# Selective-scan kernel: which engine weights each state, in a plan per scan order, and how y is laid out for two of them

## The reference, cut to what matters

```python
xs = jnp.stack([x_hw, x_wh, x_hw[..., ::-1], x_wh[..., ::-1]], axis=1)
delta = jax.nn.softplus(dts + dt_b[None, :, :, None])
def step(h, xs_t):
    d_t, u_t, B_t, C_t = xs_t
    dA = jnp.exp(d_t[..., None] * A)
    h = h * dA + (d_t * u_t)[..., None] * B_t[:, :, None, :]
    y = jnp.einsum('bkdn,bkn->bkd', h, C_t)
    return (h, y)
ys = ys[:, 0:2] + ys[:, 2:4, :, ::-1]
y = ys[:, 0] + ys[:, 1].reshape(Bb, Dd, Ww, Hh).transpose(0, 1, 3, 2).reshape(Bb, Dd, L)
```

## Time and profile before

| | us |
|---|---|
| median of 3 runs | 14696.03 |
| lowest and highest run | 14689.11, 14702.75 |
| the profiled execution | 14691.09 |
| its span | 14689.3 |
| PE, DVE, ACT, POOL busy in it | 13181.2, 12970.4, 11123.1, 10326.6 |

### The profile page before, as it was taken

The page is one execution under the profiler, slowest core; times in us unless marked ns, Lnnn a source line. Parts: engine busy times, 40 slices in busy tenths (PEclk is TensorE's granted clock), DMA queues, the critical chain, the costliest instruction groups (busy, mean ns, idle before and its releaser), DMA issues.

```text
span 14689.3 us, 247142 instructions
## 1 busy us (share of the span) xinstructions
PE 13181.2 (90%) x65256; PEld 8153.8 (56%) x65256; DVE 12970.4 (88%) x13833; ACT 11123.1 (76%) x22914; POOL 10326.6 (70%) x4126
## 2 busy tenths in 40 slices
PE   6888988889888998889988899888998889988899
PEld 4566455664556645566455664556645566455654
DVE  8999689996899978999689996899969999599995
ACT  5888578885788857887578876788767887678875
POOL 6999069980699807998079970899708996099960
PEclk9999999999999999999999999999999999999999
DMA  3443023430343303443033430344303442043420
GB/s 114 129 131 124 25 93 128 130 124 21 97 130 129 119 21 102 130 141 103 21 111 128 140 96 21 116 130 138 91 21 123 131 138 83 21 131 128 138 78 26
DMA packets 907982, 1468.60 MB, mean 100 GB/s; under 512 B 38912, under 2 KB 891904, under 8 KB 893664
## 3 DMA queue, kind: packets, MB, share of 16 engines
q1 hardware_dynamic: 906560, 1452.37, 31.2%
HBM read 1350.07 MB, written 102.17 MB: 99 GB/s over the span
## 4 chain that ended last, share of the span: by engine, by line
PE 33%; issue 24%; POOL 16%; DVE 15%; ACT 7%; DMA 2%; DVEq 1%; ACTq 1%; POOLq 0%; SPq 0%
POOL area L1794 12%; DVE area L1229 9%; PE ps L756 7%; PE ps L1030 5%; PE ps L1042 5%; DVE area L1257 4%; PE ps L743 3%; POOL area L1804 3%; PE ps L734 3%; ACT ps L1554 3%; DMA area<-bc_rows 2%; PE ps L892 2%; ACT area L1523 2%; PE ps L724 2%; PE ps L856 1%
## 5 line engine op out<-in xcount | busy, mean ns | idle before, releaser
L1229 DVE TENSOR_TENSOR_SCAN area<-ps,hst,area 128x384 f32<-128x384 f32 x9216 | 8581.8, 994 | 150.5 <-ACT ps L1554 69.6
L1794 POOL TENSOR_TENSOR area<-area 128x1152 f32<-128x1152 f32 x3072 | 7998.3, 2638 | 62.6 <-POOL area L1779 29.4
L1554 ACT ACTIVATE ps<-area,a_neg 128x384 f32<-128x384 f32 x9216 | 5259.7, 580 | 984.8 <-DVE area L1229 959.2
L756 PE MATMUL ps<-area,ident 128*128 128x384 f32 x11472 | 4127.3, 494 | 441.5 <-POOL area L1804 408.2
L756 PEld LDWEIGHTS ps<-area,ident 128*128 128x128 f32 x11472 | 2050.0, 191 | 1918.6 <-POOL area L1804 449.4
L743 PE MATMUL ps<-ident,area 128*128 128x128 f32 x20736 | 2882.2, 275 | 0.0
L743 PEld LDWEIGHTS ps<-ident,area 128*128 128x128 f32 x20736 | 2604.0, 192 | 50.3 <-ACT area L1523 1.5
L1523 ACT ACTIVATE area<-ps,area 128x384 f32<-128x384 f32 x3456 | 1972.6, 571 | 560.2 <-PE ps L734 559.4
L1714 ACT ACTIVATE area<-ps,t_neg,area 128x768 f32<-128x768 f32 x1728 | 1617.8, 986 | 1001.1 <-PE ps L1030 1001.1
L1774 POOL TENSOR_TENSOR area<-area,ones 128x2304 f32<-128x2304 f32 x16 | 85.2, 5352 | 3103.5 <-ACT area L1483 2980.9
L734 PE MATMUL ps<-ident,area 128*128 128x128 f32 x10368 | 1765.2, 279 | 326.4 <-ACT area L1523 314.0
(11 more groups left out here) (163 smaller groups left out, 9539.6 us busy)
## 6 DMA issues: line engine op xcount, KB each, us to landing
area<-bc_rows SPq DMA_DIRECT2D x1536, 768.0 KB, 6.7
xz<-x_normed SPq DMA_DIRECT2D x144, 288.0 KB, 6.3
area<-in_x SPq DMA_DIRECT2D x18, 1728.0 KB, 10.1
area<-x_padded SPq DMA_DIRECT2D x24, 1250.0 KB, 12.1
z_raw<-z_st SPq DMA_DIRECT2D x144, 192.0 KB, 6.2
area<-z_raw SPq DMA_DIRECT2D x8, 3456.0 KB, 14.9
x_padded<-x_st SPq DMA_DIRECT2D x120, 200.0 KB, 7.8
x_normed<-area SPq DMA_DIRECT2D x9, 1728.0 KB, 8.1
```

What stands on the lines that cost most here:

```text
L756: m = e.matmul(ps[:, 5 + j, 0:CH], ident[:], hb[:, i % NH, j], start=i == 0, stop=i == N - 1)
L1229: e.tensor_tensor_scan(rev(hb[:, i % NH, j], k), rev(ps[:, 2 + j, 0:CH], k), rev(dbu[:, i % NH, j], k), hst[:, i, j:j + 1], ALU.mult, ALU. ...
L1554: e.activation(ps[:, 2 + j, 0:CH], dlt[:, par, j], ACT.Exp, scale=a_neg[:, j, k, i:i + 1]).then_inc(da, 1)
L1794: e.tensor_tensor(dbu[:, i % NH], du[:, par], row_b[:, q % 2, i % ROWS:i % ROWS + 1].broadcast_to([128, J, CH]), ALU.mult).then_inc(dbus, 1)
```

## The change

The plans are new. `FIVE` (GpSimd 0, 3, 6, 9; turned 1, 4, 7, 10, 13) served orders 0 and 1; now order 1 has `SIX`, in which state 3 is turned and GpSimd has 0, 6, 9. Orders 0 and 2 have `LATE`: GpSimd 0, 6, 11; turned 1, 3, 4, 7, 10, 12, 13; so VectorE has 2, 5, 8, 9, 14, 15, and the units stand at 12 and 13 in place of 10 and 14, or 10 and 13. Order 3 keeps `SEVEN`, with GpSimd 0, 6, 9, the same turned states and VectorE 2, 5, 8, 11, 14, 15. In a late plan the x unit waits until the third delta tile has left bank 1 (dp_v), and the z unit waits for the x unit's copy-out (unit_ev).

In a slot with two tiles, the sums of GpSimd states now follow the first tile in place of leading. What was last in a slot, the add of y, and a unit that stands at 13, are done ahead of the second tile (`between`). Waits that named states 5, 8 and 11 or 8 follow the plan (`after_ln`, `ln_free`). The column orders' `y_chunk` and `y_psum` give (row, column) in place of (column, row): the SBUF side has runs of eight elements, and the PSUM side steps by 48.

```diff
@@ -72,12 +72,16 @@
         self.sum_at = {n: n + 3 for n in pool} | {n: n + 2 for n in self.dve}
         self.order = tuple(sorted(self.sum_at, key=self.sum_at.get))
         self.unit_after = tuple(max(n for n in self.dve if n < m - 1) for m in units)
+        self.late = units[0] > 11
+        self.ln_free = max(n for n in self.dve if n < 10)
+        self.after_ln = {5: 1, 8: 2, min(n for n in self.dve if n > 10): 3}
         self.np, self.nd, self.nt, self.ns = len(pool), len(self.dve), len(self.tiles), len(self.order)
 
 
-FIVE = Plan((0, 3, 6, 9), (1, 4, 7, 10, 13), (10, 14))
+SIX = Plan((0, 6, 9), (1, 3, 4, 7, 10, 13), (10, 14))
 SEVEN = Plan((0, 6, 9), (1, 3, 4, 7, 10, 12, 13), (10, 13))
-PLANS = (FIVE, FIVE, SEVEN, SEVEN)
+LATE = Plan((0, 6, 11), (1, 3, 4, 7, 10, 12, 13), (12, 13))
+PLANS = (LATE, SIX, LATE, SEVEN)
 assert 0 in PLANS[0].pool and all(p.order[0] == 0 and p.dve[:3] == (2, 5, 8) for p in PLANS)
 
 
...
@@ -483,12 +488,12 @@
 
             if k % 2 == 0:
                 return y_v[:, :, ds(pos(k, c), CH)]
-            return y_v.rearrange("p j (h w) -> p j w h", h=H)[:, :, ds(c * 8 if k < 2 else (NC - 1) * 8 - c * 8, 8), :]
+            return y_v.rearrange("p j (h w) -> p j h w", h=H)[:, :, :, ds(c * 8 if k < 2 else (NC - 1) * 8 - c * 8, 8)]
 
         def y_psum(k):
 
             p = ps[:, 5:8, 0:CH]
-            return p if k % 2 == 0 else p.rearrange("p j (w h) -> p j w h", w=8)
+            return p if k % 2 == 0 else p.rearrange("p j (w h) -> p j h w", w=8)
 
 
         @block.sync
@@ -762,33 +767,54 @@
                     if at:
                         turned_sum(q, at - 1)
 
-                def slot(q, m):
+                def slot(q, m, between=None):
 
                     p = plan(q)
-                    for i in p.order:
-                        if p.sum_at[i] == m and i in p.pool:
-                            state_sum(q, i)
+                    sums = [i for i in p.order if p.sum_at[i] == m]
+                    if len(p.slots[m]) < 2:
+                        for i in sums:
+                            if i in p.pool:
+                                state_sum(q, i)
                     for at in p.slots[m][:1]:
                         tile(q, at)
                     if m == N + 1:
                         turned_sum(q, p.nt - 1)
-                    for i in p.order:
-                        if p.sum_at[i] == m and i in p.dve:
+                    for i in sums:
+                        if i in p.dve or len(p.slots[m]) == 2:
                             state_sum(q, i)
+                    if between:
+                        between()
                     for at in p.slots[m][1:]:
                         tile(q, at)
 
+                def add_y(k, c, m):
+                    if m in ADD_AT:
+                        j = ADD_AT[m]
+                        if k == 0:
+                            e.matmul(ps[:, 5 + j, 0:CH], d_diag[:, j], u_v[:, 0, j, ds(pos(k, c), CH)],
+                                     start=False, stop=False)
+                        else:
+                            e.matmul(y_psum(k)[:, j], ident[:], y_chunk(k, c)[:, j], start=False, stop=False)
+
                 def unit(k, h, q, i):
 
                     e.wait_ge(hcs, made_d(b, q, plan(q).dve.index(plan(q).unit_after[i]) + 1))
+                    if i == 1:
+                        e.wait_ge(unit_ev, h * 2 + 1)
+                    elif plan(q).late:
+                        e.wait_ge(dp_v, b * 72 + (3 * q + 6))
                     e.wait_ge(xz_in, h * 16 + 16)
                     for t in range(CT):
                         at = i * DI + k * 128
                         m = e.matmul(ps[:, 1, 0:CH], w_in[:, t, at:at + 128], xz[:, t], start=t == 0, stop=t == CT - 1)
                     m.then_inc(unit_mm, 1)
 
+                def filler(k, c, h, q, m):
+                    add_y(k, c, m)
+                    if k < UK and m == 13 and m in plan(q).units:
+                        unit(k, h, q, plan(q).units.index(m))
+
                 def body(k, c, par, last, nxt):
-                    g = e.snap(b * 24 + (c + k * NC))
                     q = k * NC + c
                     h = e.snap(b * UC + (c + k * NC)) if k < UK else None
                     for m in range(N):
@@ -799,7 +825,7 @@
                                 e.wait_ge(ct_cp, b * GM + 3)
                             e.wait_ge(hcs, made_d(b, q, j))
                             delta_tile(*nxt, j, 1, 0 if last else 64)
-                        if k < UK and m in plan(q).units:
+                        if k < UK and m in plan(q).units and m != 13:
                             unit(k, h, q, plan(q).units.index(m))
                         if m < 2 and last:
                             slot(q - 1, N + m)
@@ -808,16 +834,9 @@
                             turn_c(1)
                             alone(e)
                             e.wait_ge(ct_cp, b * GM + GM)
-                        slot(q, m)
+                        slot(q, m, lambda: filler(k, c, h, q, m))
                         if m < 3 and m in LATE_X and not last:
                             x_proj(1, LATE_X[m])
-                        if m in ADD_AT:
-                            j = ADD_AT[m]
-                            if k == 0:
-                                e.matmul(ps[:, 5 + j, 0:CH], d_diag[:, j], u_v[:, 0, j, ds(pos(k, c), CH)],
-                                         start=False, stop=False)
-                            else:
-                                e.matmul(y_psum(k)[:, j], ident[:], y_chunk(k, c)[:, j], start=False, stop=False)
 
                 walk(e, body)
                 q = K * NC - 1
...
@@ -1505,12 +1526,12 @@
                         e.wait_ge(dp_rd, g * 3 + (3 + 1))
                     if h is not None and i == 14:
                         e.wait_ge(unit_ev, h * 2 + 2)
-                    if nxt and i in (5, 8, 11):
-                        e.wait_ge(dp_v, g * 3 + (3 + (i - 2) // 3))
+                    if nxt and i in plan(q0).after_ln:
+                        e.wait_ge(dp_v, g * 3 + (3 + plan(q0).after_ln[i]))
                     d = plan(q0).dve.index(i)
                     q = i // ROWS
                     e.wait_ge(c_in[q % 2], g * 32 + (16 * (q // 2) + 16))
-                    e.wait_ge(hcs, made_d(b, q0, d))
+                    e.wait_ge(hcs, made[q0] + d)
                     e.activation(ps[:, 1, 0:CH], row_c[:, q % 2, i % ROWS], ACT.Copy).then_inc(c_ps, 1)
 
                 def turned_product(k, c, at):
...
@@ -1576,8 +1598,8 @@
                         if k < UK and i - 1 in plan(q).units:
                             unit_out(h, plan(q).units.index(i - 1))
                         if nxt and i in LN_AT:
-                            softplus(g + 1, 1 - par, nxt[0], "ln", LN_AT[i], h=h if i == 11 else None,
-                                     c8=made_d(b, q, plan(q).dve.index(8) + 1))
+                            softplus(g + 1, 1 - par, nxt[0], "ln", LN_AT[i], h=h if i == 11 and not plan(q).late else None,
+                                     c8=made[q] + (plan(q).dve.index(plan(q).ln_free) + 1))
                         if i >= 1:
                             c_copy(g, q, i - 1, nxt, h)
                         if i == 2 and last:
```

More of the change, by code:

```diff
@@ L98 @@
 LAST = PLANS[-1]
+assert S_ALL % NC == 0 and all(not p.slots[N + 1] and max(map(len, p.slots.values())) < 3 for p in PLANS)
 def made_p(b, q, n):
@@ L117, in made_s @@
 def made_s(b, q, n):
-    return b * S_ALL + (LAST.ns + S_TO[q] + n)
+    return b * NC * (S_ALL // NC) + (LAST.ns + S_TO[q] + n)
 ADD_AT = {5: 0, 8: 1, 11: 2}
@@ L1494, in scan_phase @@
             def scan_phase(b):
+                tiles, made = {}, {}
                 def hold_state(k, c, i):
@@ L1520, in turned_product @@
                     t = c * 3 if k < 2 else (NC - 1) * 3 - c * 3
-                    e.wait_ge(turn_mm, made_t(b, q, at + 1))
-                    e.wait_ge(turn_sum, made_t(b, q, at - 2))
+                    e.wait_ge(turn_mm, tiles[q] + (at + 1))
+                    e.wait_ge(turn_sum, tiles[q] + (at - 2))
                     e.activation(ht[:, at % 3], ps[:, 0, 0:CH], ACT.Copy,
@@ L1540, in store_y @@
                         e.wait_ge(ysum, made_s(b, k * NC + c, plan(k * NC + c).ns))
-                    e.wait_ge(turn_sum, made_t(b, k * NC + c, plan(k * NC + c).nt))
+                    e.wait_ge(turn_sum, tiles[k * NC + c] + plan(k * NC + c).nt)
                     e.activation(y_chunk(k, c)[:, j], y_psum(k)[:, j], ACT.Copy).then_inc(yev, 1)
@@ L1547, in body @@
                     h = e.snap(b * UC + (c + k * NC)) if k < UK else None
+                    tiles[q], made[q] = e.snap(made_t(b, q, 0)), e.snap(made_d(b, q, 0))
                     e.wait_ge(dp_v, g * 3 + 3)
```

## The result

The changed kernel takes **14749.62 us** (median of 6 runs, 14742.95 to 14758.00) against 14697.21 (6 runs, 14689.11 to 14702.75): 1.0036 times as long, 95% interval 1.0024 to 1.0049. It is slower by 52 us, where I forecast 16 more than before and called that no change: 52 is past the 29 us from which, by the prediction's own words, a change can be told. The profiled execution took 14742.95 us, its span 14741.1. TensorE's granted clock was 0.99 of the full 2.4 GHz in it, as before, so the clock plays no part.

What follows compares the result with a forecast made beforehand. VectorE's program was taken as the scan phase's floor. Per image +2.8 +5.3 -3.0 -3.1 = +2.0 us, times eight +16 on 14,691.1, plus 5 for the median: 14,711, called no change; range 14,500 to 14,790.

Steps and rivals of the forecast that it cites:

- The new wait: First and third orders: VectorE's scan of state 15 waits for state 11's sum, 2.03 us a chunk, 12.2 an order.
- The third order: Scan phase, third order: old waits of 6.9 us go, 12.2 of waiting at state 15 come; +5.3 us per image.
- The first order: Scan phase, first order: one VectorE product fewer -7.4, old waits -2.0, waiting at state 15 +12.2; +2.8 us per image.
- The longer list of turned tiles may delay the first order: First order: more turned tiles might cause delay; unpriced, one of the unlisted things that shared a chance of 0.10.
- The second order: Scan phase, second order: GpSimd's waits go, -3.0 us per image, and the exponentials' waits go, -1.7.
- The fourth order: Scan phase, fourth order: waits for ScalarE's exponentials go, -1.4 us per image.
- y in runs of eight: Second and fourth orders: ScalarE's y stores fall to 0.49 us, waits for state 3's exponentials vanish; -3.1 us per image.
- The adds are worth nothing either way unless an add grows past 1.3 us: TensorE's adds of y, moved ahead of a slot's second tile, fill a gap of waiting for ScalarE; no gain or loss.
- the third rival: Strided PSUM side costs more than strided SBUF did: stores 1.17 us, 14,821 us in all; chance 0.10.
- The new wait does not bind: Rival: state 11's sum comes early enough, so 24.4 us per image stay away; 14,516 us, chance 0.17.
- The runs of eight change nothing: Rival: the stride costs the same in PSUM, so the waits at y's stores stay; 14,738 us, chance 0.13.
- The PSUM side is dearer: Rival: y stores with the PSUM stride take 1.17 us, delaying state 3's last exponential; 14,821 us, chance 0.10.

Runs made afterwards that it cites:

- The two experiments on the sum: Changed kernel with state 11's sum first in its slot, 14631.10 us; changed kernel with that sum cut from three tiles to one, 14633.27 us.
- that on the z unit: Changed kernel with the z unit of the first and third orders cut to one of its two matmuls: 14755.41 us.

## Why the prediction was right or wrong

**The new wait: right.** State 15 on VectorE waits for the sum of state 11 in each of twelve chunks an image. The forecast was 1.95 of idle time and 2.03 in all; it is 2.04 and 2.12. The missing 0.09 is the step from the sum's end to the scan: I put it at 0.03, a figure that no row of mine showed, and it is 0.13. The two experiments on the sum tie it to its place and its length; that on the z unit rules the unit out.

**The third order: right.** Forecast +5.3, measured +5.5; both of its terms hold: the old wait went down to 0.2 already in the kernels that have SEVEN there and the new order in a slot, and the new one is in the profile.

**The first order: mis-sized, and this is the step that failed.** Forecast +2.8, measured +6.2. I took a chunk with seven VectorE products, 53.85, and 1.24 off it, so 52.6 without the stall. I had let the three tiles of state 3 be free there, since the fourth order's waits show none from TensorE. They cost time in steps too short for that view. A clean chunk with six products is 52.86, as the fourth order after shows; 52.86 + 2.12 = 54.98, and it is 55.00. The chunk of the fourth order before held this already: 53.24 less its wait of 0.27 + 0.08 is 52.89. Its timeline shows where, from the first delta of the chunk to the second:

```profile
4905.74 0.53 DVE L1178 SCALAR_TENSOR_TENSOR area<-area,ps 128x384 f32<-128x384 f32 x1
4906.21 2.83 DVE L1229 TENSOR_TENSOR_SCAN area<-ps,hst,area 128x384 f32<-128x384 f32 x3
4909.00 1.35 DVE L1257 TENSOR_TENSOR area<-area,ps 128x1152 f32<-128x1152 f32 x1
4910.27 5.73 DVE L1229 TENSOR_TENSOR_SCAN area<-ps,hst,area 128x384 f32<-128x384 f32 x6
4915.93 0.53 DVE L1178 SCALAR_TENSOR_TENSOR area<-area,ps 128x384 f32<-128x384 f32 x1
```

That is 10.19 us. The chunk of the earlier trace rows from which I took 53.85 does the same list in 9.90:

```profile
3875.43 0.53 DVE L1178 SCALAR_TENSOR_TENSOR area<-area,ps 128x384 f32<-128x384 f32 x1
...
3879.86 5.55 DVE L1229 TENSOR_TENSOR_SCAN area<-ps,hst,area 128x384 f32<-128x384 f32 x6
3885.33 0.53 DVE L1178 SCALAR_TENSOR_TENSOR area<-area,ps 128x384 f32<-128x384 f32 x1
```

So this stretch holds the whole 0.25: most of it in the six scans, where state 8 waits, and 0.1 in the three steps ahead of them, each 0.03 to 0.04 longer (0.47, 2.79 and 1.27 from start to start, for 0.44, 2.75 and 1.24); what holds these three stays open. The changed kernel takes 10.18 there (3885.34 to 3895.52). Of the gap of 3.4, six times 0.25 for the clean chunk is 1.5, six times 0.09 on the stall 0.5, and the two new waits of the first chunk 1.3. "The longer list of turned tiles may delay the first order" stood in the prediction among the things not listed, at a chance and without a price.

**The second order: the same error.** Forecast -4.7 (-3.0 and -1.7), measured -3.1. GpSimd's waits and the exponentials' went as forecast, to none; but its chunk came to 52.86 + 1.26 for one product more, 54.12, where the forecast had 53.9: six times 0.25 again.

**The fourth order: right**, -1.6 for -1.4.

**y in runs of eight: right by its row, too small in its price.** Stores came out at 0.487 for a forecast of 0.49, and the ten waits went. I priced that at 25 us, and 27 with the third order's one; the layout taken back costs 42 with the adds in their old place. In the traces the scan phases, from the first scan to the last, take 30 of that difference (10457 us in the changed kernel, 10487 with the old layout and the adds last), close to the waits' price. Another 4 are the last chunk's stores, which end 0.51 us later in each image (8.32 us after the last scan for 7.81). The rest lies in the parts between the stores and the next image's first scan, which last 508 to 514 us whatever the kernel, so it can't be put down to the layout.

**"The adds are worth nothing either way unless an add grows past 1.3 us": right in the change, with a wrong price beside it.** The new add takes 0.81 and brings no wait. But I took a record's 0.80 for the price of the old add, which is two records and 1.45 together, past the 1.3 already. So the third rival's remark that the gap covers adds "up to twice their price now" is wrong: at their old price, between the tiles, they cost 44 us (the kernel with 48-element columns against that with the adds last). And the 0.75 of the earlier trace rows is a gap ahead of state 12's tile, where no add stands; at the adds' place 0.93 pass, of which the fast add fills 0.81.

**The rivals.** "The new wait does not bind" fell with the profile. "The runs of eight change nothing" fell with the stores. "The PSUM side is dearer" fell with the same rows: 487 ns where it needed 730. The rule in the Trainium skill (Advanced Engine Details and Errata, PSUM Cachelines), by which any non-contiguous pattern in PSUM slows matmuls significantly, is not borne out for these float32 matmuls: 486 ns contiguous and 486 to 488 with a step of 48.

In sum, +16 became +52 mostly because two orders were built on a clean chunk that was 0.25 us too short: 12 x 0.25 = 3.0 an image, 24 us. The first chunk's 1.3 make 10 more, and the 0.09 on twelve stalls 9. Together that is 43 where the medians lie 36 past the forecast; the parts outside the scan phases, which the forecast left as they were, came out 8 us shorter in the trace, which is about the difference. The time lies inside the 14,670 to 14,755 that I gave my own case, but by luck: I drew that range from 0.4 us on each new wait, and these missed by 0.09.

## What to carry to other kernels

A step moved later on an in-order engine is priced by its end: find who writes the buffer that it reads last, and set the end against that writer's due time. Four engines' busy times said nothing of the 2 us here; the chain was worked out from an undisturbed stretch of another order and was right to 0.1 us. When a part of the work takes a form that another part already has, take its whole measured length as the base, and don't build it from pieces: waits under the profile's threshold are in the whole and not in the pieces.

## What the runs showed of the hardware

A step of 48 float32 elements costs TensorE 0.32 us per record of 384 elements when it reads them from SBUF (802 ns for 486), so 0.64 per matmul of two records (1.45 us for 0.81), and nothing when it writes them to PSUM (486 to 488 ns). It costs ScalarE up to 0.37 us when it writes them to SBUF (862 ns for 487), and nothing when it reads them from PSUM (467 to 492 ns). Runs of eight on the SBUF side are as fast as contiguous rows on both engines, by the same figures.
